# Layer 1 attention of a four-layer kernel: the products of the heads on GpSimd in halves, VectorE sums them, and a new order of the instructions of layers 0 to 2

## The reference

```python
xn = _layernorm(x, axis=-1)
s = _L1_attn_ref(xn, ...)         # layer 1: attention among the 16 heads of one token
g = _silu(_L1_ffn_ref(xn, ...))   # layer 1: mixture of 8 experts, 2 of them chosen
x = x + s * g
```

## Time and profile before

| | us |
|---|---|
| median of 3 runs | 3261.69 (3253.01 to 3262.71) |
| the profiled execution | 3271.89 |
| its span | 3270.0 |
| mean granted TensorE clock over the span | 0.848 of full speed |

### The profile page before, as it was taken

One profiled execution on the slowest core, in us unless ns is written; L12 is line 12 of the kernel. 1 busy time (PEld: TensorE's weight loads), 2 busy tenths in 40 slices (PEclk: granted clock), 3 DMA queues, 4 the chain that ended last, 5 costly groups with the idle time before them and its releaser, 6 DMA issues.

```text
span 3270.0 us, 39867 instructions
## 1 busy us (share of the span) xinstructions
PE 2397.1 (73%) x13593; PEld 1314.4 (40%) x13729; DVE 2549.4 (78%) x5554; ACT 1633.7 (50%) x3182; POOL 521.0 (16%) x530
## 2 busy tenths in 40 slices
...
DMA packets 312997, 286.90 MB, mean 88 GB/s; under 512 B 16504, under 2 KB 286474, under 8 KB 311226
## 3 DMA queue, kind: packets, MB, share of 16 engines
...
## 4 chain that ended last, share of the span: by engine, by line
DVE 41%; PE 32%; ACT 14%; issue 8%; DMA 3%; SPq 2%; POOL 1%; DVEq 0%; POOLq 0%; ACTq 0%
PE banks L2642 5%; PE banks L2688 4%; DVE t L2618 3%; DVE t L1017 2%; ACT t L2629 2%; PE banks L2602 2%; DVE t L1169 2%; DVE t L952 2%; ACT L144 1%; ACT t L2553 1%; DVE t L2673 1%; PE banks L1085 1%; ACT t L1395 1%; DVE t L1700 1%; DVE t L1704 1%
## 5 line engine op out<-in xcount | busy, mean ns | idle before, releaser
L2618 DVE CUSTOM_DVE_ANT_0 t<-banks,t 128x640 f32<-128x640 f32 (+7 forms) x512 | 378.1, 748 | 179.4 <-PE banks L2642 70.5
L2629 ACT ACTIVATE t<-t 128x640 f32<-128x640 f32 (+7 forms) x512 | 390.9, 780 | 92.8 <-DVE t L2618 92.0
L2642 PE MATMUL banks<-ident,t 128*128 128x128 f32 x2304 | 362.7, 283 | 47.1 <-DVE t L2839 17.7
L2642 PEld LDWEIGHTS banks<-ident,t 128*128 128x128 f32 x2304 | 255.9, 143 | 114.0 <-ACT t L2629 56.1
L2602 PE MATMUL banks<-t 128*128 128x512 bf16 (+3 forms) x640 | 169.9, 328 | 76.7 <-DVE t L2618 37.1
L2585 POOL TENSOR_TENSOR t<-t 128x512 f32<-128x512 f32 x96 | 122.3, 1274 | 638.0 <-DMA t<-relative_scratch 601.8
L2673 DVE COPY t<-banks 128x512 f32<-128x512 f32 x256 | 175.7, 686 | 32.9 <-PE banks L2642 32.1
L548 POOL TENSOR_TENSOR t<-t 128x512 f32<-128x512 f32 x28 | 48.1, 1718 | 916.9 <-ACT t L520 916.9
L1085 PE MATMUL banks<-t 128*128 128x512 f32 x256 | 145.1, 650 | 42.9 <-DVE t L1165 32.2
L1740 ACT ACTIVATE t<-t 128x16 f32<-128x16 f32 x256 | 82.5, 322 | 184.5 <-DVE t L1704 142.8
L1119 ACT ACTIVATE t<-banks 128x512 f32<-128x512 f32 x128 | 76.5, 597 | 193.6 <-PE banks L1085 193.4
...
## 6 DMA issues: line engine op xcount, KB each, us to landing
relative_scratch<-t SPq DMA_DIRECT2D x128, 512.0 KB, 3.6
t<-relative_scratch SPq DMA_DIRECT2D x128, 512.0 KB, 5.2
relative_scratch<-t SPq DMA_DIRECT2D x128, 256.0 KB, 4.5
...
```

Source lines behind the costliest of these rows:

```text
L2618: nc.vector.tensor_tensor_reduce(s.s[z][:, 0:n], ps[:, b0:b0 + 1 + i // 4, :].rearrange("p b n -> p (b n)")[:, 0:n], s.bias[r][:, j, WIDE ...
L2629: nc.scalar.activation(s.s[z][:, 0:n], s.s[z][:, 0:n], ACT.Exp, scale=-1.0, bias=s.least[:, z:z + 1]).then_inc(*a.mark("weights", u))
L2642: nc.tensor.transpose(ps[:, 4 + c % 2, (t - lo) * P:(t - lo + 1) * P], s.s[u % NS][:, t * P:(t + 1) * P], k.ident[:]).then_inc(*e.mark("tu ...
```

## The change

A new part att1_pool puts the products on GpSimd. Each tile's 2048 products are two instructions of 1024 (half j of the heads), and each half of `prod` is written again when VectorE has summed it. att1_dve keeps the sums, also in halves, and waits for each product. The other engines wait for the second half of s_tok where they waited for the whole. The strings of all five engines are written anew, so the order of every part of layers 0 to 2 may differ. Behind the change, lines of att1_dve and of all that follows have other numbers: L1169 is L1193, L1165 is L1189, L1654 and L1656 are L1678 and L1680, L1649 and L1650 are L1673 and L1674, L1661 is L1685, L1675 to L1688 are L1699 to L1712, L1602 to L1621 are L1626 to L1645, L1010 is L1038.

```diff
--- before.py
+++ after.py
@@ -893,7 +893,7 @@
         yield
         for line, *key in free("heads_out", u):
             pe.wait_ge(line, *key)
-        pe.wait_ge(v, "s_tok", u, t)
+        pe.wait_ge(v, "s_tok", u, t, 1)
         nc.tensor.transpose(ps[:, bk, t * P:(t + 1) * P], o.s_tok[:, t], k.ident[:]).then_inc(*e.mark("s_tok", u))
 
 
@@ -904,7 +904,7 @@
         yield
         act.wait_ge(e, "qkv", u, t)
         if u:
-            act.wait_ge(v, "s_tok", u - 1, NT - 1)
+            act.wait_ge(v, "s_tok", u - 1, NT - 1, 1)
         nc.scalar.activation(o.qkv[:, t, 0:D], bank(ps, bk, D), ACT.Copy, scale=ATTN_SCALE1).then_inc(*a.mark())
         nc.scalar.copy(o.qkv[:, t, D:], ps[:, bk, D:3 * D]).then_inc(*a.mark("qkv", u, t))
     yield
@@ -931,8 +931,40 @@
     nc.scalar.copy(s.s_T[:], bank(ps, bk)).then_inc(*a.mark("s_T", u))
 
 
+def halved(x, j):
+    n = x.shape[1] // 2
+    return x[:, j * n:(j + 1) * n]
+
+
+def att1_pool(k, s, u):
+
+    nc, pool, (e, a, v), o, g = k.nc, k.pool, att1_lines(k), s.att, k.line("att1_pool")
+    for t in range(NT):
+        q = o.qkv[:, t, 0:D].rearrange("p (h d) -> p h d", h=NH)
+        kk = o.qkv[:, t, D:2 * D].rearrange("p (h d) -> p h d", h=NH)
+        for j in range(2):
+            yield
+            pool.wait_ge(a, "qkv", u, t)
+            if t:
+                pool.wait_ge(v, "scores", u, t - 1, j)
+            elif u:
+                pool.wait_ge(v, "s_tok", u - 1, NT - 1, j)
+            nc.gpsimd.tensor_tensor(halved(o.prod, j).rearrange("p (h g d) -> p h g d", h=NH // 2, g=NH), rep(halved(q, j), 2, NH),
+                                    rep(kk, 1, NH // 2), ALU.mult).then_inc(*g.mark("scores", u, t, j))
+    for t in range(NT):
+        x = o.qkv[:, t, 2 * D:].rearrange("p (d g) -> p d g", g=NH)
+        w = o.z[:, t].rearrange("p (h g) -> p h g", h=NH)
+        for j in range(2):
+            yield
+            pool.wait_ge(a, "weights", u)
+            if t:
+                pool.wait_ge(v, "s_tok", u, t - 1, j)
+            nc.gpsimd.tensor_tensor(halved(o.prod, j).rearrange("p (h d g) -> p h d g", h=NH // 2, d=HD), rep(halved(w, j), 2, HD),
+                                    rep(x, 1, NH // 2), ALU.mult).then_inc(*g.mark("values", u, t, j))
+
+
 def att1_dve(k, s, u):
-    nc, dve, (e, a, v), o = k.nc, k.dve, att1_lines(k), s.att
+    nc, dve, (e, a, v), o, g = k.nc, k.dve, att1_lines(k), s.att, k.line("att1_pool")
     tt, ts, reduce, copy = nc.vector.tensor_tensor, nc.vector.tensor_scalar, nc.vector.tensor_reduce, nc.vector.tensor_copy
     rows = NT * NH
     prod = o.prod
@@ -942,17 +974,13 @@
         tt(o.masked, s.xn1[:].rearrange("p (t n) -> p t n", t=NT), rep(s.before[:], 1, NT), ALU.mult).then_inc(*v.mark("masked", u))
     yield
     if u:
-        dve.wait_ge(a, "weights", u - 1)
+        dve.wait_ge(v, "s_tok", u - 1, NT - 1, 1)
     for t in range(NT):
-        q = o.qkv[:, t, 0:D].rearrange("p (h d) -> p h d", h=NH)
-        kk = o.qkv[:, t, D:2 * D].rearrange("p (h d) -> p h d", h=NH)
-        yield
-        dve.wait_ge(a, "qkv", u, t)
-        dve.wait_ge(v)
-        tt(prod.rearrange("p (h g d) -> p h g d", h=NH, g=NH), rep(q, 2, NH), rep(kk, 1, NH), ALU.mult).then_inc(*v.mark())
-        yield
-        dve.wait_ge(v)
-        reduce(o.z[:, t], prod.rearrange("p (x d) -> p x d", d=HD), AX, ALU.add).then_inc(*v.mark())
+        for j in range(2):
+            yield
+            dve.wait_ge(g, "scores", u, t, j)
+            reduce(halved(o.z[:, t], j), halved(prod, j).rearrange("p (x d) -> p x d", d=HD), AX, ALU.add).then_inc(
+                *v.mark("scores", u, t, j))
     yield
     dve.wait_ge(v)
     flat, r3 = "p t g -> p (t g)", "p t (h g) -> p (t h) g"
@@ -1009,15 +1037,11 @@
     dve.wait_ge(v)
     tt(z, z, rep(one, 2, NH), ALU.subtract).then_inc(*v.mark("weights", u))
     for t in range(NT):
-        x = o.qkv[:, t, 2 * D:].rearrange("p (d g) -> p d g", g=NH)
-        w = o.z[:, t].rearrange("p (h g) -> p h g", h=NH)
-        yield
-        dve.wait_ge(a, "weights", u)
-        dve.wait_ge(v)
-        tt(prod.rearrange("p (h d g) -> p h d g", h=NH, d=HD), rep(w, 2, HD), rep(x, 1, NH), ALU.mult).then_inc(*v.mark())
-        yield
-        dve.wait_ge(v)
-        reduce(o.s_tok[:, t], prod.rearrange("p (x g) -> p x g", g=NH), AX, ALU.add).then_inc(*v.mark("s_tok", u, t))
+        for j in range(2):
+            yield
+            dve.wait_ge(g, "values", u, t, j)
+            reduce(halved(o.s_tok[:, t], j), halved(prod, j).rearrange("p (x g) -> p x g", g=NH), AX, ALU.add).then_inc(
+                *v.mark("s_tok", u, t, j))
     yield
     dve.wait_ge(k.line("moe1_act"), "out", u)
     dve.wait_ge(a, "s_T", u)
@@ -1808,71 +1832,72 @@
...
 TURNS_POOL = (
-    "mcmmmmccccccccccccccccccmmmmccccccccccccccccccmmmmccccccccccccccccccmmmmccccccccccccccccccmmmmcccccccccccccccccc"
...
+    "macaaaaaaaamaaaaaaamammcccaaacaaaaaccccccccccccccmaaaaaamaammcccaaacaaaaaccccccccccccccmaaaaaaamammcccaaacaaaaac"
...
@@ -1956,7 +1981,8 @@
...
-    in_turn(TURNS_POOL, {"mixer": every(lambda u: mixer_pool(k, s, u)), "turns": every(lambda u: turns_pool(k, s, u))})
+    in_turn(TURNS_POOL, {"mixer": every(lambda u: mixer_pool(k, s, u)), "att1": every(lambda u: att1_pool(k, s, u)),
+                         "turns": every(lambda u: turns_pool(k, s, u))})
```

More of the change, by code:

```diff
@@ L1810 @@
 TURNS_PE = (
[L1811 to L1820, removed]
@@ new lines @@
+    "emmememmmemmeemeemeeebeeeeeememmmmmmmeememeeebeaaaaiiimmmmmmmmimmimiimmmmmmmmimmiimmimeemettettmtttetmgegeaaeeae"
+    "aeaefmeeeemfeeffeffeffmffeeemeeemeeeeffeeemmeeefffemmememmmemmeemeemeeebeeeeeememmmmmmmeememeeebeaaaaiiimmmmmmmm"
+    "immimiimmmmmmmmimmiimmimeemettettmtttetmgegeaaeeaeaeaefmeeeemfeeffeffeffmffeeemeeemeeeeffeeemmeeefffemmememmmemm"
+    "eemeemeeebeeeeeememmmmmmmeememeeebeaaaaiiimmmmmmmmimmimiimmmmmmmmimmiimmimeemettettmtttetmgegeaaeeaeaeaefmeeeemf"
+    "eeffeffeffmffeeemeeemeeeeffeeemmeeefffemmememmmemmeemeemeeebeeeeeememmmmmmmeememeeebeaaaaiiimmmmmmmmimmimiimmmmm"
@@ L1836 @@
-    "rrriiiiiiiiiiiiiiigigigttgtggttggtttkkbbrrrrrrrrrrrrrrrrrrrrrrrrrrrrrrrrbb"
+    "gmmfktiearbmmmfmmmmmmmfffffmmmmmffmfmfmfmmmmmmmmmmmmmmemmeeamammeaaefmmmeefmfeefaefefmmeeamaffmmeeaaffemfiemmeee"
+    "mmemaeimiimimiiiiiimmimmiimmiimiieiieeimiggmgmttettgggttegtgtmkkmmaeamaeafeemffemffemfaeemamamffmmeeaaffemfiemme"
+    "eemmeaermririirirrmrrmrmriirririririrmimrmmrririrrrririrmrmriirmrririemeieimmgggttettgtggtegtgtmkkmmaeamaeafmeef"
+    "ffefmfemaeeffamammmmffefiaeaeemmbemeemmerbrerarmririirirrmrrmrmriirririririrmimrmmrririrrrririrmrmriirmiimeiimme"
@@ new lines @@
+    "egggttttgegtgtmgtgtemkmkeaeaaafmeemfffefmfemaeeffamammmmffefiaeaeemmbemeemmerbrerarmririirirrmrrmrmriirririririr"
+    "mimrmmrririrrrririrmrmriirmiimeiimmeegggttttgegtgtmgtgtemkmkeaeaaafmeemfffefmfemaeeffamammmmffefiaeaeemmbemeemme"
+    "rbrerarmririirirrmrrmrmriirririririrmimrmmrririrrrririrmrmriirmiimeiimmeegggttttgegtgtmgtgtemkmkeaeaaafmeemfffef"
+    "mfemaeeffamammmmffefiaeaeemmbemeemmerbrerarmririirirrmrrmrmriirririririrmimrmmrririrrrririrmrmriirmiimeiimmeeggg"
+    "ttttgegtgtmgtgtemkmkeaeaaafmeemfffefmfemaeeffamammmmffefiaeaeemmbemeemmerbrerarmririirirrmrrmrmriirririririrmimr"
@@ new lines @@
+    "fafeaafafmafafamfafefmrmfafefmmfemafrfafmfafafefmfeemamrrarieaamrmreeamreraeremrmrmamremareerrrraraarrrrrrmrrrrr"
+    "rrrirrimrmrrrrmrrrrrrmrmrrrrrrrrrrmrrrrrrrrrrrrrrrrirrririmimiririrrrrrrmrrrrrrrrrrrrrrirrrrrrrrrrrrrrrrrrrirrrr"
+    "rrrrrmrrirrrrmrmrmmrrrrrrrrrrgrririrrriririregrgrggmgegegegegegemgemeeeggggggggggefrrrmrrraeraaefefffafffafeafea"
+    "efaaafafaaaafaffafeafafafafaaeafaeafafmaffmefrfrfefmamfefmfmamfararmaeirerreamrmemaamrmeearaerbmeaerarmammerbrmb"
+    "mrrreerrrrrrrrrrrraraarrrrrrmrrrrrrrrirrimrmrrrrmrrrrrrmrmrrrrrrrrrrmrrrrrrrrrrrrrrrrirrririmimiririrrrrrrmrrrrr"
@@ new lines @@
+    "rrrrrrrrrirrrrrrrrrrrrrrrrrrrirrrrrrrrrmrrirrrrmrmrmmrrgririrriririrgegmggggegegegegegegegemggemggeggggfemrrrrre"
+    "raeraafefffffafefafaaeefaaafafaaaafaffafeafafafafaaeafaeafafmaffmefrfrfefmamfefmfmamfararmaeirerreamrmemaamrmeea"
+    "raerbmeaerarmammerbrmbmrrreerrrrrrrrrrrraraarrrrrrmrrrrrrrrirrimrmrrrrmrrrrrrmrmrrrrrrrrrrmrrrrrrrrrrrrrrrrirrri"
+    "rimimiririrrrrrrmrrrrrrrrrrrrrrirrrrrrrrrrrrrrrrrrrirrrrrrrrrmrrirrrrmrmrmmrrgririrriririrgegmggggegegegegegegeg"
+    "emggemggeggggfemrrrrreraeraafefffffafefafaaeefaaafafaaaafaffafeafafafafaaeafaeafafmaffmefrfrfefmamfefmfmamfararm"
```

66 lines of the change are left out of this document (27 added, 39 removed).

## The result

The changed kernel takes 3358.57 us (median of 4 runs, 3352.74 to 3361.57) against 3262.2 us (median of 4, 3253.01 to 3271.78) for the kernel before, measured beside it: a ratio of 1.0286 (95% interval 1.0264 to 1.0308). It is slower by 96 us.

What follows compares the result with a forecast made beforehand. VectorE, busy 94% of a period in layers 0 to 2, was the bound. +16.2 us a unit less 6.5 of waits, +9.7 over seven periods, +68 on 3271.9, less 10: 3330 us; range 3200 to 3375, likeliest case 3290 to 3375.

Steps and rivals of the forecast that it cites:

- The exclusion: VectorE instructions with two SBUF inputs and GpSimd's products exclude each other: stalls of 12.2 us (scores), 11.4 us (values) a unit.
- GpSimd's product: Each of sixteen 1024-element products a unit on GpSimd was to take 2.48 us, 39.7 us a unit.
- the walk: Going through VectorE's changed order for one unit, with assumed instruction lengths, to find which instructions GpSimd's products stall.
- The turn chain moves: GpSimd's turn chain now meets VectorE's sorting network: +12 us a unit, less 0.5 that small products no longer lose.
- Its waits for them shrink: A later VectorE lets the other engines get ahead, so its waits for them shrink by 6.5 us a period.
- the new order of the other engines I cost at nothing: Reordering the other engines costs 0 us, hidden by TensorE's 51 us of idle time a period.
- The sum: All terms in layers 0 to 2: +16.2 us a unit, less 6.5 of waits, +9.7 us a period.
- The first unit ... I count it nothing.: The first unit, with 47 us of idle VectorE in 202, was to add 0 us.
- A: Rival: reordering pairs GpSimd's products with VectorE work that does not clash; 3200 us, chance 0.26.
- B: Rival: no difference, cover of 30 to 37 us and shrunken waits even out; 3262 us, chance 0.08.
- D: Rival: no lock for these shapes, VectorE sheds 17.7 us a unit; 3120 us, chance 0.03 inside another rival's.
- C: Rival: the mixer's L548 on GpSimd waits behind products, TensorE's state products wait for it; 3385 us, chance 0.08.

Runs made afterwards that it cites:

- memset: The changed kernel with each GpSimd product replaced by three fills that write SBUF and read nothing, layer 1's attention products left out: 3199.19 us, ratio 0.9802 to before.
- short_chain: The changed kernel with 30 of the 41 GpSimd turn chain instructions a unit left out: 3300.39 us, ratio 1.01 to the kernel before.
- short_before: The kernel before with 30 of the 41 GpSimd turn chain instructions a unit left out: 3242.43 us, ratio 0.9935 to before.
- order_only: The kernel before, all products on VectorE, with the changed kernel's order tables for TensorE, ScalarE, VectorE and SyncE: 3313.21 us, ratio 1.0146 to before.
- sums_ahead: The kernel before with the sums of the value products moved straight behind their products on VectorE, no work added: 3319.51 us, ratio 1.0175 to before.

## Why the prediction was right, and where it was not

3330 us was forecast, 3358.57 measured, inside the range (3200 to 3375) and the likeliest case's own. The exclusion was right in kind and nearly in size; the chain's term was mis-sized, and the term of the waits had the wrong sign. Of the signs that it named, most came: a period of 228.7 us (225 forecast), L807 and L808 above 0.69 us, executions of L1680 and L1708 2 us too long.

- **The exclusion.** Right, and shown by memset: VectorE's stalls are 18.4 us of busy time a period, to which 1.1 us of waiting for the seventh product come. The forecast had 12.2 + 11.4 - 1.2 = 22.4 with that wait in it. Among the values the walk hit nearly each stall, one of them at L1709 in place of the first L1705 (2.1 + 2.1 + 1.9 + 1.0 + 1.8 + 1.8 = 10.7 and 0.6 at L610, against 11.4); L1680's 1.8 too. Of the scores only L1673 with L1674 (4.2 for 4.8), L1680 and L301 (1.6) were there: L283 and L289, ahead of which VectorE waits 3.2 us for ScalarE at L280, were not held; the walk did not have that wait. To tie it to two SBUF inputs was too narrow, though: L295, a TENSOR_SCALAR with one, takes 2.43 us at 614.87 beside a L952, and 0.43 alone. The Trainium skill (SBUF — State Buffer, "Who interferes with whom") limits the exclusion of an instruction with two SBUF inputs to GpSimd instructions that read SBUF; the traces agree, with 2.281 us for L1686 of memset beside fills.
- **GpSimd's product** is 2.33 us, not the 2.48 scaled from the earlier trace rows. The Trainium skill (GPSIMD Engine Reference, "Performance versus the Vector engine") gives 4497 ns for 2048 elements; half of it, 2.25 us, was the nearer estimate, and I had set it aside.
- **"The turn chain moves", +12 us less 0.5.** Mis-sized. Of the busy time, -18.9 + 1.1 + 18.4 leave 4.5 us of the measured 5.1 for the chain and all else, and some 4.9 us can be read off the grown instructions of the period; in the length of the period the move is worth some 8 us, an estimate from short_chain and short_before, waits that follow included. The fault was to charge every GpSimd instruction in full: L807 and L808 alternate with chain instructions of 0.2 to 0.66 us, and 15.3 us of them raised the twenty L807 and L808 of a period from 0.68 us to 0.83 and 0.91 in the mean, 3.7 us. That it is the chain which raised them, order_only shows: there it does not meet them, and they have 0.69 and 0.68 us (medians). Why short ones hold VectorE for so much less than their recorded time was not taken apart.
- **"Its waits for them shrink", -6.5 us.** Wrong in sign: the idle time grew, by 8.4 us in the period shown and by 5.7 in the mean of seven. Bound to it was "the new order of the other engines I cost at nothing, because TensorE has 51 us of idle time a period to hide it". order_only prices that order alone at 51 us, 4.7 of idle time a period. TensorE's idle time did not hide it, since what counts is when it gets its input: sums_ahead shows that placing four sums ahead of what releases TensorE and ScalarE costs 57 us without any work. That the same mechanism makes each of the changed kernel's waits (L280, L591, L1189) I conclude from this and did not test one by one, and what the lower granted clock adds stays open.
- **The sum.** Forecast +16.2 of busy time and -6.5 of waits, +9.7 a period; measured +5.1 and +8.4, +13.6 (rounded apart). Two errors of 11 and 15 us against each other left one of 4, times seven 27 us. So the hit is luck in good part: with the measured +8.4 for the waits, its own sum would have come to 24.6 us a period and some 3434 us, 75 too many.
- **"The first unit ... I count it nothing."** Right, as the start of the first recurrence product shows. The 9.4 us that the end is shorter (1400.5 for 1409.9) the forecast did not have.
- **Rivals.** A fell: the order pairs some products well, but 18 us of stalls remain. B fell with the time. D fell with the stalls. C fell in its form: no instruction of TensorE is seen to wait for L548 in the changed kernel's trace. With fills that read nothing in place of the products the kernel is 2% faster than before (memset), so in this order the lock decides the sign.
